# Attention with the scores and values of two steps made together in every second step, and PSUM banks laid out anew

## What is computed

```
def local_attention(q, k, v):          # w = WINDOW = 32
    ...
    bk2, bv2 = (look(bk), look(bv))    # own and preceding window: 64 keys
    ...
    sim = jnp.einsum('bhwie,bhwje->bhwij', bq, bk2) * QK_SCALE
    sim = jnp.where(mask, -jnp.finfo(sim.dtype).max, sim)
    attn = jax.nn.softmax(sim, -1)
    out = jnp.einsum('bhwij,bhwje->bhwie', attn, bv2)
```

## Time and profile before

| | us |
|---|---|
| median of the runs | 2067.97 |
| lowest and highest of three | 2062.97, 2070.41 |
| the profiled execution | 2066.36 |
| its span, first to last instruction | 2064.6 |

### The profile page before, as it was taken

One profiled execution on the slowest core, in us unless ns is written; L12 is line 12 of the kernel. 1 busy time (PEld: TensorE's weight loads), 2 busy tenths in 40 slices (PEclk: granted clock), 3 DMA queues, 4 the chain that ended last, 5 costly groups with the idle time before them and its releaser, 6 DMA issues.

```text
span 2064.6 us, 82312 instructions
## 1 busy us (share of the span) xinstructions
PE 1989.6 (96%) x33044; PEld 1399.8 (68%) x33044; DVE 1518.1 (74%) x2875; ACT 1383.4 (67%) x4164; POOL 1225.6 (59%) x1374
## 2 busy tenths in 40 slices
PE   7789798999999999999999999999999999999998
PEld 3333233887686786876876877868768778687684
DVE  1499897886796776867867967769678678686783
ACT  4533233886786777767867867768678677776783
POOL 1376774775584565765746855648557567565570
PEclk9888989999999999999999999999999999999999
DMA  1321110311131111121211311112211111111110
GB/s 62 134 72 70 63 61 0 105 44 38 39 90 42 40 43 39 45 77 36 53 37 37 96 38 41 44 32 50 76 47 43 40 39 49 38 43 33 24 40 22
DMA packets 148091, 104.30 MB, mean 51 GB/s; under 512 B 15778, under 2 KB 140256, under 8 KB 146176
## 3 DMA queue, kind: packets, MB, share of 16 engines
q1 hardware_dynamic: 147712, 99.07, 17.3%
HBM read 48.31 MB, written 1.18 MB: 24 GB/s over the span
## 4 chain that ended last, share of the span: by engine, by line
PE 82%; issue 0%; POOL 0%; ACT 0%; DVE 0%; POOLq 0%; ACTq 0%
PE ps L1033 20%; PE ps L1040 9%; PE ps L1019 8%; PE ps L1058 8%; PE ps L1000 8%; PE ps L981 7%; PE ps L1054 4%; PE ps L958 4%; PE ps L1098 3%; PE ps L1092 3%; PE ps L1103 3%; PE ps L975 2%; PE ps L1078 1%; PE ps L1087 1%; PE ps L1133 0%
## 5 line engine op out<-in xcount | busy, mean ns | idle before, releaser
L1510 POOL TENSOR_TENSOR QK<-QK,RN 128x512 f32<-128x512 f32 x384 | 400.8, 1044 | 374.2 <-ACT RN L1223 359.1
L1233 ACT ACTIVATE PR<-ps,MN 128x64 f32<-128x64 f32 x1536 | 357.3, 316 | 154.6 <-DVE MN L1361 139.8
L1033 PE MATMUL ps<-W,XS 128*128 128x256 f32 x1536 | 435.3, 406 | 4.9 <-PEq L64 4.1
L1505 POOL TENSOR_TENSOR QK<-PC,PS 128x256 f32<-128x256 f32 x384 | 280.7, 731 | 246.4 <-PE ps L1019 243.7
L1259 ACT COPY QKT<-ps 128x512 f32<-128x512 f32 x384 | 225.0, 586 | 248.6 <-PE ps L1019 248.6
L1385 DVE TENSOR_REDUCE SS<-SQ 128x8 f32<-128x512 f32 x384 | 262.3, 683 | 58.0 <-ACT SQ L1266 55.2
L1033 PEld LDWEIGHTS ps<-W,XS 128*128 128x128 f32 x1536 | 261.0, 189 | 61.5 <-issue 4.9
L1506 POOL TENSOR_TENSOR QK<-PC,PS 128x256 f32<-128x256 f32 x384 | 281.3, 733 | 0.0
L1361 DVE TENSOR_REDUCE MN<-ps 128x4 f32<-128x256 f32 x384 | 163.0, 424 | 149.8 <-PE ps L981 148.5
L1404 DVE TENSOR_TENSOR PC<-ps,TC 128x512 f32<-128x512 f32 x384 | 261.4, 681 | 0.1
L1406 DVE TENSOR_TENSOR PS<-ps,TS 128x512 f32<-128x512 f32 x384 | 260.7, 679 | 0.0
(11 more groups left out here) (142 smaller groups left out, 3226.7 us busy)
## 6 DMA issues: line engine op xcount, KB each, us to landing
V<-V SPq DMA_DIRECT2D x384, 97.5 KB, 2.2
scr<-B_rows SPq DMA_DIRECT2D x32, 512.0 KB, 3.5
V<-V SPq DMA_DIRECT2D x288, 32.5 KB, 2.4
W<-in_Wqkv SPq DMA_DIRECT2D x40, 192.0 KB, 2.8
TC<-in_tcos SPq DMA_DIRECT2D x6, 1024.0 KB, 5.9
TS<-in_tsin SPq DMA_DIRECT2D x6, 1024.0 KB, 8.5
WO<-in_Wo SPq DMA_DIRECT2D x6, 512.0 KB, 4.1
W<-in_W SPq DMA_DIRECT2D x6, 341.0 KB
```

Of the source, the lines that this page charges most:

```text
L1033: mm = nc.tensor.matmul(ps[:, par, k * 2 * P:(k + 1) * 2 * P], cols[k], W[:, i, 0:2, :].rearrange("p t m -> p (t m)"), start=True, stop=True)
L1233: e = nc.scalar.activation(PR[:, m % 2, h, slot * DH:(slot + 1) * DH], ps[:, 3 + h, slot * DH:(slot + 1) * DH], ACT.Exp, scale=-1.0, bias= ...
L1505: nc.gpsimd.tensor_tensor(QK[:, par, :, 0:hd], PC[:, par, :, 0:hd], PS[:, par, :, hd:DH], ALU.add)
L1510: nc.gpsimd.tensor_tensor(QK[:, par, :, :], QK[:, par, :, :], bcast_last(RN[:, m // 2 % 2, 8 * par:8 * par + 8], DH), ALU.mult).then_inc(q ...
```

## The change

The scores and the values of two steps, an even one and the odd one after it, are made in one go in every even row; odd rows have neither. In an even row n PE now has scores of steps n-6 and n-5 and values of n-8 and n-7. The mask products take 256 columns instead of 128, one per head for both steps. The transposes of q and k of both steps are in the even row as well, the second four between the projection of q and k and that of v. The projection of v moves from bank 5 to bank 4 and is a function of its own (`project_v`); the transposed probabilities of the two heads go to the ends of banks 5 and 6, the transposed output to the end of bank 3.

With the second step's scores made as early as the first's, the first step's exponentials come one row later than before and the output copy too; the pipeline is one row longer, and all work between rows is shifted by one row (`U_WO` and the others; the feed-forward network now follows the odd row 17).

On DVE one `least` covers both steps (512 scores per query row set), and one reciprocal both, followed by two multiplications. `clamp_pair` and `tables` stand ahead of `least` and `normalise`.

On ACT even rows are `copy_qk`, `norm_pair`, `exponents`, `copy_out`, `squares`, `copy_v`; odd rows are `exponents`, `copy_p` of the even row's probabilities, `copy_qk`, `copy_out`, `squares`, `copy_v`, `copy_p`.

Several waits are new, among them `v_cp` ahead of the second output transpose of an odd row, `oT_ps` ahead of the odd row's exponentials, and `pr` ahead of every projection of v. The diff, cut to its core:

```diff
@@ PE @@
             def out_transposed(n):
-                m = n - 8
+                m = n - 9
...
                 pe.wait_ge(on, m + 1)
                 for k in range(2):
+                    if steady(n) and n % 2 == 1 and k == 1:
+                        pe.wait_ge(v_cp, n)
                     src = ON[:, m % 2, :, :].rearrange("p (k h) d -> p k (h d)", k=2)[:, k, :]
-                    mm = nc.tensor.transpose(ps[:, 3, (1 + k) * P:(2 + k) * P], src, ident[:])
+                    mm = nc.tensor.transpose(ps[:, 3, (2 + k) * P:(3 + k) * P], src, ident[:])
...
             def scores(n):
-                m = n - 5
...
+                if n % 2 or not 0 <= n - 6 < NSTEPS:
+                    return
...
-                    nc.tensor.matmul(ps[:, 3 + h, 0:P], identb[:], MASKB[:, int(s == 0), h, :], start=True, stop=True)
+                    nc.tensor.matmul(ps[:, 3 + h, 0:2 * P].rearrange("p (f c) -> p f c", f=2), identb[:],
+                                     MASKB[:, f:f + 2, h, :], start=True, stop=True)
...
+                for m in (n - 6, n - 5):
...
             def values(n):
-                m = n - 7
...
+                if n % 2 or not 0 <= n - 8 < NSTEPS:
...
+                pe.wait_ge(pT, n - 6)
+                for m in (n - 8, n - 7):
...
             def project(n):
...
                 for k in range(2):
+                    if k == 1 and n % 2 == 0:
+                        wait(pe, mn, n - 4)
...
+            def project_v(n):
...
-                wait(pe, on, n - 6)
+                wait(pe, pr, n - 5)
                 for k in range(2):
-                    mm = nc.tensor.matmul(ps[:, 5, (2 + k) * P:(3 + k) * P], cols[k], W[:, i, 2, :], start=True, stop=True)
+                    if steady(n) and n % 2 == 1 and k == 1:
+                        pe.wait_ge(pT, n - 6)
+                    mm = nc.tensor.matmul(ps[:, 4, (2 + k) * P:(3 + k) * P], cols[k], W[:, i, 2, :], start=True, stop=True)
                 mm.then_inc(v_ps, 1)
...
-                qk_transposed(n)
+                if n % 2 == 0:
+                    qk_transposed(n)
                 out_transposed(n)
                 scores(n)
                 values(n)
                 project(n)
+                if n % 2 == 0:
+                    qk_transposed(n + 1)
+                project_v(n)
                 p_transposed(n)
@@ ACT @@
             def exponents(n):
-                m = n - 5
+                m = n - 6
...
+                if m % 2:
+                    wait(act, oT_ps, min(n - 8, NSTEPS))
...
-                norm_pair(n)
-                copy_qk(n)
-                exponents(n)
+                if n % 2 == 0:
+                    copy_qk(n)
+                    norm_pair(n)
+                    exponents(n)
+                    copy_out(n)
+                    squares(n)
+                    copy_v(n)
+                else:
+                    exponents(n)
+                    copy_p(n - 1)
+                    copy_qk(n)
...
-                else:
+                elif n % 2:
                     copy_out(n)
                     squares(n)
+                    copy_v(n)
                     copy_p(n)
-                    copy_v(n)
@@ DVE @@
             def least(n):
-                m = n - 5
...
+                if n % 2 or not 0 <= n - 6 < NSTEPS:
+                    return
+                dve.wait_ge(s_ps, n - 4)
...
-                                        AX.X, ALU.min).then_inc(mn, 1)
+                                        AX.X, ALU.min).then_inc(mn, 2)
...
+                clamp_pair(n)
+                tables(n)
                 least(n)
                 normalise(n)
-                clamp_pair(n)
-                tables(n)
                 norms(n)
```

More of the change, by code:

```diff
@@ L987, in values @@
             def values(n):
-                m = n - 7
-                if not 0 <= m < NSTEPS:
+                if n % 2 or not 0 <= n - 8 < NSTEPS:
                     return
                 if not steady(n):
[L992 to L1000, removed]
-                                              PT[r, m % 2, h, 32 * quad:32 * quad + 32],
-                                              V[r, 2 * (m % 8) + j // 4, 2 * (1 - j % 2) + h, :], start=True, stop=True)
@@ L1003, in values @@
-                mm.then_inc(o_ps, 1)
+                    for m in (n - 8, n - 7):
+                        pe.wait_ge(v_sh[m % 4], 32 * (m // 4 + 1))
+                    wait(pe, on, n - 8)
+                pe.wait_ge(pT, n - 6)
+                for m in (n - 8, n - 7):
+                    for h in range(2):
+                        for slot, quad in spread_tiles:
+                            j = window(slot, quad)
+                            r = slice(64 * slot, 64 * slot + 64)
+                            o0 = (2 * (m % 2) + h) * (DH + 1)
+                            mm = nc.tensor.matmul(ps[32 * quad:32 * quad + 32, 5 + slot, o0:o0 + DH + 1],
+                                                  PT[r, m % 2, h, 32 * quad:32 * quad + 32],
+                                                  V[r, 2 * (m % 8) + j // 4, 2 * (1 - j % 2) + h, :], start=True, stop=True)
+                    mm.then_inc(o_ps, 1)
@@ L1008, in qk_transposed @@
                     return
-                if not steady(n):
+                if not steady(n) or n % 2:
                     wait(pe, qkT, m)
@@ L1013, in qk_transposed @@
                     for k in range(2):
[L1014 to L1017 removed]
+                        if steady(n) and n % 2 == 0 and (x, k) == (1, 0):
+                            pe.wait_ge(oT, n - 9)
                         src = QK[:, m % 2, :, :].rearrange("p (k x h) d -> p k x (h d)", k=2, x=2)[:, k, x, :]
@@ L1048, in p_transposed @@
                     wait(pe, pT, m)
-                    wait(pe, on, m)
                     pe.wait_ge(pr, m + 1)
+                wait(pe, on, min(n - 6 - n % 2, NSTEPS))
                 for h in range(2):
-                    if h == 1 and 7 <= n < NSTEPS - 1:
+                    if h == 1 and n % 2 and 7 <= n < NSTEPS - 1:
                         pe.wait_ge(qkT, n - 3)
-                    mm = nc.tensor.transpose(ps[:, 6, (2 + h) * P:(3 + h) * P], PR[:, m % 2, h, :], ident[:])
+                    if h == 1 and n % 2 == 0 and steady(n + 1):
+                        pe.wait_ge(oT, n - 8)
+                    mm = nc.tensor.transpose(ps[:, 5 + h, 3 * P:4 * P], PR[:, m % 2, h, :], ident[:])
                 mm.then_inc(pT_ps, 1)
```

118 lines of the change are left out of this document (61 added, 57 removed).

## The result

| | us |
|---|---|
| before, median | 2067.97 |
| after, median of three (lowest, highest) | 2333.7 (2333.45, 2334.94) |
| ratio, with its 95% interval | 1.129 (1.126 to 1.133) |
| span of the profiled execution | 2333.1 |

The account below looks back on a forecast made before the run. PE bounded the kernel before; a closed ring of 7.9 us per pair against 6.56 would bound the new one. Blocks 220, first block 16, end 3: together 238 us on 2066.4, about 2300 us; range 2180 to 2390.

Parts of the forecast that it names:

- the ring: Closed chain from odd-row squares through tables, `least`, exponentials, v, its copy, output transpose and back: 7.93 us per pair; chance 0.63.
- the hops: Gaps from released work's end to next start: 0.04 us DVE to ACT, PE to ACT, ACT to DVE; 0.21 into PE.
- what PE saves: PE's own instructions in a pair of rows: 0.4 to 0.5 us less, so PE alone would need about 6.1 us.
- the 0.15 for the scores: On PE, a second batch of scores right behind the first costs 0.23 us, not 0.38: 0.15 saved per pair.
- The values and the return to the whole array: On PE: values save 0.04 to 0.12 us; one of two returns from small tiles, about 0.18 each, goes.
- the work between rows: Output projections, means, logarithms and residual additions between rows: -2 us per block, between -5 and +2, an estimate.
- between 0 and +1 each for three places, partly given back: Residual additions ahead of table products, and so of `least`, in DVE's queue: cost in us at three places per block.
- the groups for the means: PE's four mean and variance groups per block, now falling into PE's waits: -3.5 us.
- Half the ring: Rival: squares to `least` come early enough, PE sets the even row; 7.3 us per pair, about 2185 us; chance 0.12.
- The clock: Rival: PE's waits lower its granted clock in the attention, adding 30 to 95 us, 2330 to 2395; chance 0.16.
- The faster case: Rival: all waits end before PE arrives, PE bounds at 6.1 us per pair, 1980 us; chance 0.06.
- No change: Rival: PE's save and the ring cancel within 6 us, leaving the time within 0.3%; chance 0.03.

Follow-up runs that it names:

- the three kernels with the copy of v first: Odd rows copy v before output copy and squares: changed kernel alone 2401.09 us; with tables and v-copy wait also moved 2239.99; that plus both exponentials in even rows 2237.19.
- values twice, one behind the other: The kernel before, with the 16 products of the values made twice in each row, the second time over the first; 2200.81 us.
- values behind the projection: The changed kernel with its values moved behind the projection of q and k, so not right behind the scores; 2503.54 us.
- the first experiment: The changed kernel with DVE's two table products of a row moved behind `least` and the division, the clamp staying in front; 2273.8 us, ratio 1.101.
- both edits: The changed kernel with tables behind `least`, and the v-copy wait moved from odd row's second output transpose to its projection of v; 2239.52 us, ratio 1.085.

## Why the prediction was right and wrong

**Right: the ring and its size.** The forecast was a closed ring of 7.93 us per pair; it measures 7.82, and the edges are the named ones. In the pair shown above: squares to sums 0.70 (1606.66 to 1607.36), sums to table products 0.83 (to 1608.19; 0.80 was said), table products to `least` 1.20, `least` to exponentials 0.71 (1601.56 to 1602.27), exponentials to v products 0.99 (to 1603.26), to the copy of v 0.73 (to 1603.99), to the odd exponentials 0.88 (to 1604.87), to the next squares 1.79 (to 1606.66). The sum is 7.83. `least` over 512 scores took 0.67; taking the sum over 512 squares as its price was right. Between the first chain and the next one under it lay only 0.17 us, and that the followed ring was the longer of the two wasn't worked out: in this there was some luck.

**Right in sum, wrong in the hops.** I took 0.21 for ACT to PE from a single place. It was no hop: PE had no gap there in its chain, and over the whole kernel before, the weight load of v that waits for the division (L1040) starts 0.053 after it (median). From the exponentials' end to v it is 0.06 (1603.20 to 1603.26), which makes 0.15 less; from the copy's end to the end of the transpose it is 0.38 (1604.37 to 1604.75), where 0.48 was said. From the transposes to the exponentials it is 0.12 where 0.04 was said, and the v group lasts 0.70, not 0.61. Together these make the 0.1 us between 7.93 and 7.82; that they nearly cancel is luck.

**Mis-sized: what PE saves.** This step said 0.4 to 0.5 us per pair (its own terms add up to 0.37 to 0.45), so that PE alone would need 6.1 us. I measure it from the first mask product to the start of the projection, in medians of the starts. Plain rows of before take 0.99 us, two of them 1.99. In the changed kernel there are two cases. In 57 of the 188 pairs the masks follow the output transposes without a wait, and the stretch takes 1.73. In the others, the pair shown above among them, PE is held for the copy of v right ahead of the masks, and then the stretch behind the wait takes 1.97. In the three kernels with the copy of v first, where nothing holds PE right ahead of the masks, the median is 1.73 for all pairs. By parts:

| us, from start to start | before, two rows | after, not held | after, held |
|---|---|---|---|
| first mask product to first score | 0.41 | 0.31 | 0.32 |
| first score to first value | 0.53 | 0.61 | 0.71 |
| first value to the projection | 1.05 | 0.81 | 0.94 |
| all | 1.99 | 1.73 | 1.97 |

So the merge saves 0.25 us of PE's time by itself, about half of what was said, and 0.02 in the pairs that are held. The values and the return to the whole array save 0.24, as said (0.22 to 0.30). The masks save 0.10, for which nothing was put. The term that failed is the 0.15 for the scores: they take 0.07 more. Its 0.23 was the spread of the starts of 32 scores, and I read it as PE's pace, which it is for the first 32 only:

| batch of 64 | first 32 start over, us | the other 32 |
|---|---|---|
| scores, after, held | 0.238 | 0.467 |
| scores, after, not held | 0.238 | 0.375 |
| values, after, held | 0.312 | 0.462 |
| values, after, not held | 0.331 | 0.332 |
| values twice, one behind the other | 0.357 | 0.332 |
| values behind the projection | 0.245 | 0.377 |

(0.376 for the 32 values of the kernel before, which have 32 scores ahead of them.) PE's instructions then fill about 6.3 us of a pair, 6.56 less 0.25, and not the 6.54 that an expectation took from the held pairs. This didn't move the forecast, since the ring left PE waiting in either case. With no ring over 6.3 us the merge could win at most 0.25 us in each of 190 pairs, 48 us, an estimate from these medians. None of the versions above is faster than the kernel before, and one without such a ring wasn't made.

**Wrong in sign: the work between rows.** I put it at -2 us per block, within -5 to +2; it is +1.7. The term that I had sized "between 0 and +1 each for three places, partly given back" is the one that the experiments show: by the first of them each of the three costs 1.0 us in full, 3 per block, since the additions stand ahead of the table products and `least` in the same queue, on the ring. What the groups for the means gave back, put at 3.5, wasn't measured by itself. The eleven blocks cost 22.2 each in the mean, 244 us where 220 was said; in this the pair's 0.11 works the other way. The first block costs 18.3 (99.0 to 117.3; 16 was said), and from the last squares to the end of the span it is 7 more (60.5 to 67.8; up to 3 was said). With the 1.2 us by which the attention starts earlier, these make the 268.5 that the spans differ by, 30 more than the 238 of the sum.

**An edge not seen: the masks.** The masks' wait for the odd row's copy of v closes a second ring, by way of scores, values, projection, v, copy of v, output transpose, exponentials, three copies, squares and copy of v. The prediction doesn't name it. It was 7.65 by the first experiment, 0.17 under the ring that I followed, so the forecast didn't suffer; the experiments' expectations did, three times over. Part of its length goes with the wait itself: PE stands still for 0.2 us ahead of the masks, and the stretch behind takes 0.24 longer than where it isn't held.

**The rivals.** Half the ring: `least` waits for PE only twice, so it isn't the changed kernel's case; taken by force in the first experiment, it gave 7.65 per pair, not 7.3, because I had ended that ring at the last probability transpose and not at the masks. The clock: 1.00, though PE waits in every pair. The rule of the Trainium skill in "TensorE: Matmul & The Clock Gate", section "A second HAM failure mode: psum-queue depth-cycling", would have it go up and down here; by that rule, the trace disagrees. The faster case fell with the ring, and PE's saving was half of what it counted on. No change: the two would have had to cancel.

## What to carry to other kernels

Before instructions of a full engine are regrouped, follow every new wait until it comes back to its start: the length of that ring over the rows that it spans is a floor for the period, and it can be read from the rows of the kernel before, here to 0.1 us, though errors in the hops cancelled in it. Look also for the rings just below it, since removing one edge gains only the distance to the next; a serial engine's queue order counts as an edge like any wait. The profile's chain may follow the shorter of two such rings when they differ by little, as here, so cut one and see what is left. A wait right ahead of a long batch of small products can cost more than its own length. And don't take the spread of a short batch's starts for an engine's pace: measure a batch twice as long.

## What was not expected of the hardware

Of the small tiled products (64 rows by 32 columns, 64 or 65 columns moving), the first 32 of a batch start mostly 6 to 7 ns apart, 32 scores in 0.238 us. Then come two gaps of 78 and 56 ns behind the 33rd and the 34th weight load (pair at 1600 of the changed kernel), and the rest start 10 to 15 ns apart in the mean: 32 in 0.33 to 0.47 us. The fast start shows in the scores of both kernels and in the values behind the projection; values that have scores right ahead of them start more slowly (0.31 to 0.38 us for the first 32). Where PE was held for a semaphore right ahead of the masks, the later products of both batches come more slowly, with further gaps in the weight loads (84 and 134 ns in that pair): the same 64 scores and 64 values lose 0.24 us. Why wasn't measured. The Trainium skill, in "TensorE: Matmul & The Clock Gate", section "Back-to-back issue gap", speaks of a window of 64 instructions; 32 loads with their 32 products are as many, and the trace agrees in that the pace breaks there. That the window is full at the start and refilled more slowly is my reading of it; no run shows it. What sets the slower pace wasn't measured.

The time from the end of an instruction to the start of the one that waited for it is steady at the waits of the two rings, if the right start is taken (medians): 0.05 us from ACT or DVE to PE's weight load; 0.03 from DVE to ACT and from ACT to DVE; 0.04 from PE to ACT, but 0.12 from the output transposes to the odd row's exponentials (168 times). From ACT's exponentials to the first v product itself it was 0.05 in the changed kernel and 0.14 in the kernels with both edits. A single row, and the product in place of its load, is a poor source for such a term.
